# Key and value projection: context halves turned by transposing DMAs instead of fp32 transposes on TensorE

## The chip, the cores and the metric

The kernel runs on one core of a Trainium2 chip, in one launch. The metric is the device time of the launch in microseconds (us), lower is better. Matmuls run on TensorE (PE in the profile), elementwise work on VectorE (DVE), ScalarE (ACT) and GpSimd (POOL); SyncE (SP) issues all the transfers in the part that matters here.

## What is computed

The reference is one layer of a perceiver on 512 latent rows of width 512 and a context of 8192 rows of width 384: a cross attention with 16 heads, an MLP, a local self attention, and a feed-forward part with weights quantised to fp4. The change touches only the projection of the context to keys and values:

```python
k = (y @ Wk + bk).reshape(B, M, NUM_HEADS, HEAD_DIM)   # y: 8192 x 384, Wk, Wv: 384 x 512
v = (y @ Wv + bv).reshape(B, M, NUM_HEADS, HEAD_DIM)
```

## The kernel before

**Stages.** Four stages follow each other: project (keys, values, queries, and the fp4 weights on the side), attend (the cross attention), local (the self attention), ffn. The change is in project alone.

**Blocks.** The 8192 context rows are cut into NB = 16 blocks of 512 rows, y[:, u] of 128 partitions by 4 rows by 384, with u = block mod 2. Two blocks make one turn of a loop, which stands out of line for the first and the last pair and in a hardware loop (Fori) for pairs 1 to 6. fp32 accuracy is kept by splitting each operand in two fp16 halves, hi and lo, and adding three products: hi·hi, hi·lo, lo·hi.

**One block on each engine.** TensorE needs the context with its 384 columns on the partitions. In `turn_y` (line 588) it turns a block with 12 transposes of 128x128 in fp32 (line 593) into the PSUM tensor yT_ps. ACT copies yT_ps to yT_hi in fp16 (`y_high`, line 458), DVE subtracts to get yT_lo (`y_low`, line 513). `keys` (lines 611 to 613) then does 36 matmuls of 512 columns in four groups g; ACT writes each group as kf and k_hi (lines 449, 451), DVE makes k_lo (line 509). `values` (lines 627 to 629) does 36 more, and ACT copies each v out (line 465). TensorE's order is keys of block b, transposes of block b+1 (`next_y`), values of block b.

**Buffers.** yT_hi and yT_lo have two slots; k_ps and v_ps two banks each; yT_ps one set of three banks.

**SP's queue.** For a block, `block_dmas` (line 336) issues, in this order: the load of y for block b+2 (line 340, once block b's slot u is free), after a wait for all k_hi and k_lo of the block eight stores to k_scratch (lines 347, 348), and after a wait for the four v the store to v_scratch (line 350). After the second block of a pair come three stores and three loads of the fp4 side work (lines 361, 357). All are on one queue, q1.

**Side work.** DVE and POOL quantise the feed-forward weights in units (`scales`, `rounder`, `add`, `subtract`, `halves`), spread between DVE's k_lo and y_lo steps. It is why DVE reaches a k_lo late in some blocks.

**A transfer of the same kind.** In the local stage SP issues six transposing transfers (line 1434), each turning a 1408x512 fp16 matrix (1.44 MB) from DRAM into SBUF.

Of the kernel before, what the change touches and what calls it, by code (L numbers as in the profile page):

```python
# [22 lines left out]
ALU = mybir.AluOpType  # L23
# [3 lines left out]
F16 = mybir.dt.float16  # L27
# [102 lines left out]
def perceiver(nc, a, out):  # L130

    with ExitStack() as whole:
# [111 lines left out]
        with ExitStack() as st:  # L244
# [10 lines left out]
            yT_hi = sb("yT_hi", [P, 2, CK, BLK], F16)  # L255
            yT_lo = sb("yT_lo", [P, 2, CK, BLK], F16)
# [12 lines left out]
            w_whole = sb("w_whole", [P, UN])  # L269
            w_out = sb("w_out", [P, 3, 2, UN], F16)  # L270

            yT_ps = ps("yT_ps", [P, CK, BLK])
            k_ps = ps("k_ps", [P, 2, BLK])
            v_ps = ps("v_ps", [P, 2, D])

# [19 lines left out]
            yT_ready = sem("yT_ready")  # L295
            yhi_ready = sem("yhi_ready")
            ylo_ready = sem("ylo_ready")
            k_ready = sem("k_ready")
# [25 lines left out]
            def _(sp):  # L324
# [8 lines left out]
                sp.dma_start(y[:, 1], y_view[1]).then_inc(y_in[1], 16)  # L333
                sp.dma_start(b2[:], a["L0_xattn_b2"].partition_broadcast(P)).then_inc(b2_in, 16)

                def block_dmas(i, u, last):
                    if not last:

                        wait(sp, yT_ready, 2 * i + u + 1)
                        sp.dma_start(y[:, u], y_view[2 * i + u + 2]).then_inc(y_in[u], 16)  # L340

                    wait(sp, klo_ready, (2 * i + u + 1) * G)
                    wait(sp, khi_ready, (2 * i + u + 1) * G)
                    for s in range(HG):
                        rows = slice(s * HD, (s + 1) * HD)
                        keys = bass.ds((2 * i + u) * BLK, BLK)
                        sp.dma_start(k_hi_view[s, :, :, keys], k_hi[rows, u]).then_inc(k_out[u], 16)
                        sp.dma_start(k_lo_view[s, :, :, keys], k_lo[rows, u]).then_inc(k_out[u], 16)
                    wait(sp, vs_ready, (2 * i + u + 1) * BT)
                    sp.dma_start(v_view[:, :, bass.ds((2 * i + u) * BT * HD, BT * HD)],  # L350
                                 v[:, u].rearrange("p h t d -> p h (t d)")).then_inc(v_out[u], 16)
# [12 lines left out]
                for w in range(3):  # L364
                    sp.dma_start(w_in[:, w], w_flat[w][:, 0:UN]).then_inc(w_unit_in[w], 16)
                sp.dma_start(wq[:], a["L0_xattn_Wq"].rearrange("(k p) n -> p k n", p=P)).then_inc(wq_in, 16)
                def two_blocks(i):
                    block_dmas(i, 0, False)
                    block_dmas(i, 1, False)
                    for w in range(3):  # L370
                        unit_store(i, w)
                        unit_load(i + 1, w)
# [5 lines left out]
                for i in range(HG):  # L378
# [2 lines left out]
                    sp.dma_start(heads[0:HD, i], q_hi[rows]).then_inc(q_stacked, 16)  # L381
                    sp.dma_start(heads[HD:2 * HD, i], q_hi[rows]).then_inc(q_stacked, 16)
                    sp.dma_start(heads[2 * HD:3 * HD, i], q_lo[rows]).then_inc(q_stacked, 16)
                with sp.Fori(1, NB // 2 - 1) as i:
                    two_blocks(i)
                block_dmas(NB // 2 - 1, 0, True)
                block_dmas(NB // 2 - 1, 1, True)
# [42 lines left out]
            def _(act):  # L430
                layer_norm_scalar(act, var_ready, sd_ready, 1)

                act.wait_ge(yT_ready, 1)
                nc.scalar.activation(yT_hi[:, 0], yT_ps[:], ACT.Copy).then_inc(yhi_ready, 1)
# [18 lines left out]

                def y_high(i, u):

                    wait(act, yT_ready, 2 * i + u + 2)
                    wait(act, v_ready, (2 * i + u) * BT)
                    nc.scalar.activation(yT_hi[:, 1 - u], yT_ps[:], ACT.Copy).then_inc(yhi_ready, 1)

                def values_out(i, u):  # L460
                    for t in range(BT):
# [27 lines left out]
            def _(dve):  # L489
# [6 lines left out]
                nc.vector.tensor_tensor(yT_lo[:, 0], yT_ps[:], yT_hi[:, 0], ALU.subtract).then_inc(ylo_ready, 1)  # L496
# [88 lines left out]

            @block.tensor
            def _(pe):
                def turn_y(b, u):

                    pe.wait_ge(y_in[u], b)  # L590
                    for t in range(BT):
                        for c in range(CK):
                            last = nc.tensor.transpose(yT_ps[:, c, t * P:(t + 1) * P], y[:, u, t, c * P:(c + 1) * P],
                                                       ident[:])
                    last.then_inc(yT_ready, 1)

                pe.wait_ge(x_in, 32)
                turn_y(16, 0)
                pe.wait_ge(wsplit_hi, 1)
                pe.wait_ge(wsplit_lo, 1)  # L600

                def keys(i, u):
                    wait(pe, yhi_ready, 2 * i + u + 1)
                    wait(pe, ylo_ready, 2 * i + u + 1)
                    for g in range(G):
                        n = (2 * i + u) * G + g

                        wait(pe, khi_ready, n - 1 if g >= 2 else (2 * i + u) * G)
                        cols = slice(g * P, (g + 1) * P)
                        for k in range(CK):  # L610
                            nc.tensor.matmul(k_ps[:, g % 2], w_hi[:, 0, k, cols], yT_hi[:, u, k], start=k == 0, stop=False)  # L611
                            nc.tensor.matmul(k_ps[:, g % 2], w_hi[:, 0, k, cols], yT_lo[:, u, k], start=False, stop=False)  # L612
                            last = nc.tensor.matmul(k_ps[:, g % 2], w_lo[:, 0, k, cols], yT_hi[:, u, k], start=False,  # L613
                                                    stop=k == CK - 1)
                        last.then_inc(k_ready, 1)

                def values(i, u):
                    if isinstance(i, int) and i == 0 and u == 0:
                        pe.wait_ge(wsplit_hi, 2)
                        pe.wait_ge(wsplit_lo, 2)  # L620
                    for t in range(BT):
                        n = (2 * i + u) * BT + t

                        wait(pe, vs_ready, n - 1 if t >= 2 else (2 * i + u) * BT)
                        cols = slice(t * P, (t + 1) * P)
                        for k in range(CK):
                            nc.tensor.matmul(v_ps[:, t % 2], yT_hi[:, u, k, cols], w_hi[:, 1, k], start=k == 0, stop=False)  # L627
                            nc.tensor.matmul(v_ps[:, t % 2], yT_hi[:, u, k, cols], w_lo[:, 1, k], start=False, stop=False)  # L628
                            last = nc.tensor.matmul(v_ps[:, t % 2], yT_lo[:, u, k, cols], w_hi[:, 1, k], start=False,  # L629
                                                    stop=k == CK - 1)  # L630
                        last.then_inc(v_ready, 1)

                def next_y(i, u):
                    wait(pe, ylo_ready, 2 * i + u + 1)

                    turn_y(16 * (i + 1 + u), 1 - u)
# [12 lines left out]
                for k in range(DK):  # L649
                    if k >= 2:  # L650
                        pe.wait_ge(turned_out, k - 1)
                    for t in range(TT):
                        last = nc.tensor.transpose(v_ps[:, k % 2, t * P:(t + 1) * P], xn_q[:, t, k * P:(k + 1) * P], ident[:])
                    last.then_inc(turned, 1)
                pe.wait_ge(turned_out, DK)
                pe.wait_ge(wq_in, 16)
                for g in range(G):
                    if g >= 2:
                        pe.wait_ge(qhi_ready, g - 1)
                    for k in range(DK):  # L660
# [8 lines left out]
                next_y(i, 0)  # L669
                values(i, 0)  # L670
                keys(i, 1)
                values(i, 1)
# [1286 lines left out]
```

## Time and profile before

| | |
|---|---|
| median of 3 runs | 1485.82 us (1484.34 to 1488.38) |
| profiled execution | 1484.56 us, of which the span is 1482.8 us |
| mean granted TensorE clock | 0.955 |
| busy share of the span: PE, DVE, ACT, POOL | 91%, 76%, 55%, 54% |
| project stage in the span | from 0 to about 330 us |
| 12 transposes of a block on TensorE | 1.47 us busy |
| transfers of queue q1 | 129264 packets, 138.08 MB |

The engines run side by side, so busy shares don't add. The share of an engine is a mean over stages that differ; what counts for the change is what TensorE does, and waits for, between 8 and 321 us. Matmul durations overlap in the records (0.38 us each, started every 0.215 us), so the pitch of their starts is read, not the duration.

### The profile page before, as it was taken

The page shows a single profiled execution, that of the slowest core. Times are in us where ns is not written, and L with a number is a line of the kernel's source. Part 1 is how long each engine was busy: PE and PEld are TensorE (multiplying, and loading weights), DVE is VectorE, ACT ScalarE, POOL GpSimd, SP SyncE. Part 2 cuts the span into 40 slices and gives each one's busy share as a digit, 9 for nine tenths or more (in the row PEclk, how much of TensorE's full clock was granted, in tenths as well). Part 3 has the DMA queues.
Part 4 walks back from the last instruction along what each step waited for, and adds up shares of the span by engine and source line. Part 5 has one row for each costly group of instructions (what it writes and reads, how often), then busy time and mean ns, then how long its engine had stood idle before and what let it go on. Part 6 is the DMA issues. An engine that isn't in the chain of part 4 may idle for free. (4 is left out here: it accounts for less than half of the span.)

```text
span 1482.8 us, 43758 instructions
## 1 busy us (share of the span) xinstructions
PE 1356.4 (91%) x16736; PEld 651.1 (44%) x16736; DVE 1123.3 (76%) x1834; ACT 808.7 (55%) x1529; POOL 799.0 (54%) x307
## 2 busy tenths in 40 slices
PE   6999999968999999999999999999999897885898
PEld 3444444421344444444444444444444443453444
DVE  7477777768888887887887878878886654676797
ACT  3454444430566776666766766767667722474211
POOL 2122222232599898997997988979987001100111
PEclk9999999985899999999999999999999998898899
DMA  6578787765033222122212212221210030770000
GB/s 232 166 199 224 211 227 215 226 170 148 22 125 89 71 69 67 36 70 69 70 36 71 68 40 60 68 67 36 70 57 27 4 135 0 165 155 1 0 8 22
DMA packets 129452, 140.76 MB, mean 95 GB/s; under 512 B 44848, under 2 KB 110256, under 8 KB 127216
## 3 DMA queue, kind: packets, MB, share of 16 engines
q1 hardware_dynamic: 129264, 138.08, 32.8%
q8 instruction: 139, 2.28, 0.6%
q14 instruction: 49, 0.40, 0.1%
HBM read 77.23 MB, written 44.17 MB: 82 GB/s over the span
## 5 line engine op out<-in xcount | busy, mean ns | idle before, releaser
L1168 DVE TENSOR_REDUCE attend_part_max<-attend_banks 128x1 f32<-128x512 f32 x1024 | 635.9, 683 | 132.0 <-PE attend_banks L903 130.3
L1131 ACT ACTIVATE attend_prob<-attend_banks 128x512 f32<-128x512 f32 x1024 | 531.4, 603 | 234.9 <-PE attend_banks L955 229.6
L1316 POOL TENSOR_TENSOR early<-early,attend_prob 128x1024 f32<-128x1024 f32 x210 | 618.8, 2947 | 34.8 <-ACT attend_prob L1131 5.9
L903 PE MATMUL attend_banks<-attend_k_stack,attend_q_pre 96*32 96x512 f16 x4096 | 423.4, 401 | 31.1 <-DMA attend_k_stack<-k_scratch 16.4
L955 PE MATMUL attend_banks<-attend_q_now,attend_k_stack 97*32 97x512 f16 x4096 | 362.2, 386 | 14.3 <-ACT attend_prob L1131 14.3
L966 PE MATMUL attend_banks<-attend_prob,attend_vh 128*32 128x512 f32 x2048 | 265.2, 594 | 0.0
L955 PEld LDWEIGHTS attend_banks<-attend_q_now,attend_k_stack 97*32 97x32 f16 x4096 | 112.2, 97 | 164.1 <-ACT attend_prob L1131 104.5
L903 PEld LDWEIGHTS attend_banks<-attend_k_stack,attend_q_pre 96*32 96x32 f16 x4096 | 112.4, 96 | 126.6 <-DVE attend_part_max L1168 39.2
L977 PEld LDWEIGHTS attend_banks<-attend_prob,ones 128*32 128x32 f32 x3048 | 87.5, 109 | 159.5 <-issue 159.5
L977 PE MATMUL attend_banks<-attend_prob,ones 128*32 128x128 f32 x3048 | 126.9, 272 | 0.0
L413 POOL TENSOR_TENSOR project_w_whole<-project_grid,project_qscale 128x704 f32<-128x704 f32 x24 | 35.5, 1481 | 128.7 <-DVE project_grid L538 128.7
L1312 POOL TENSOR_TENSOR early<-attend_prob 128x1536 f32<-128x1536 f32 x15 | 53.4, 3559 | 89.6 <-ACT attend_prob L1131 89.6
L407 POOL TENSOR_TENSOR project_qn<-early,project_qinv 128x704 f32<-128x704 f32 x24 | 41.8, 1740 | 97.6 <-DVE project_qinv L524 94.1
L449 ACT ACTIVATE project_kf<-project_k_ps,project_bk 128x512 f32<-128x512 f32 x64 | 44.0, 687 | 86.1 <-PE project_k_ps L613 47.8
L627 PE MATMUL project_v_ps<-project_w_hi,project_yT_hi 128*128 128x512 f16 x192 | 73.6, 383 | 11.8 <-ACT project_v L465 11.8
L611 PE MATMUL project_k_ps<-project_yT_hi,project_w_hi 128*128 128x512 f16 x192 | 73.5, 383 | 6.8 <-DVE project_w_lo L499 5.0
L966 PEld LDWEIGHTS attend_banks<-attend_prob,attend_vh 128*32 128x32 f32 x2048 | 62.6, 111 | 35.5 <-issue 4.7
L612 PE MATMUL project_k_ps<-project_yT_lo,project_w_hi 128*128 128x512 f16 x192 | 73.6, 383 | 0.0
L628 PE MATMUL project_v_ps<-project_w_lo,project_yT_hi 128*128 128x512 f16 x192 | 73.5, 383 | 0.0
L629 PE MATMUL project_v_ps<-project_w_hi,project_yT_lo 128*128 128x512 f16 x192 | 73.4, 382 | 0.0
L613 PE MATMUL project_k_ps<-project_yT_hi,project_w_lo 128*128 128x512 f16 x192 | 73.4, 382 | 0.0
L465 ACT ACTIVATE project_v<-project_v_ps 128x512 f32<-128x512 f32 x64 | 37.7, 601 | 63.0 <-PE project_v_ps L629 63.0
(160 smaller groups left out, 1423.5 us busy)
## 6 DMA issues: line engine op xcount, KB each, us to landing
v_scratch<-project_v SPq DMA_DIRECT2D x16, 1024.0 KB, 5.7
attend_k_stack<-k_scratch SPq DMA_DIRECT2D x64, 256.0 KB, 3.5
attend_vh<-v_scratch SPq DMA_DIRECT2D x16, 1024.0 KB, 5.2
early<-in_ctx_dram SPq DMA_DIRECT2D x16, 768.0 KB, 7.4
k_scratch<-project_k_hi SPq DMA_DIRECT2D x64, 128.0 KB, 2.7
k_scratch<-project_k_lo SPq DMA_DIRECT2D x64, 128.0 KB, 2.9
attend_k_stack<-k_scratch SPq DMA_DIRECT2D x64, 128.0 KB, 3.5
late<-in_L_xattn_W_dram SPq DMA_DIRECT2D x2, 2048.0 KB, 10.7
```

Source lines behind the costliest of these rows:

```text
L611: nc.tensor.matmul(k_ps[:, g % 2], w_hi[:, 0, k, cols], yT_hi[:, u, k], start=k == 0, stop=False)
L612: nc.tensor.matmul(k_ps[:, g % 2], w_hi[:, 0, k, cols], yT_lo[:, u, k], start=False, stop=False)
L613: last = nc.tensor.matmul(k_ps[:, g % 2], w_lo[:, 0, k, cols], yT_hi[:, u, k], start=False, stop=k == CK - 1)
L627: nc.tensor.matmul(v_ps[:, t % 2], yT_hi[:, u, k, cols], w_hi[:, 1, k], start=k == 0, stop=False)
L628: nc.tensor.matmul(v_ps[:, t % 2], yT_hi[:, u, k, cols], w_lo[:, 1, k], start=False, stop=False)
L903: last = nc.tensor.matmul(pre_ps[c * HD:(c + 1) * HD, bank, :], q_pre[0:KROWS, s, queries], k_stack[0:KROWS, s, part * BLK:(part + 1) * BL ...
L955: last = nc.tensor.matmul(s_ps[c * HD:(c + 1) * HD, s_bank[n], :], k_stack[0:KROWS + 1, s, keys], q_now[0:KROWS + 1, s, :], start=True, st ...
L966: last = nc.tensor.matmul(pv_ps[t * HD:(t + 1) * HD, :], vh[:, s, BT * q + t, :], prob[:, q % PSLOTS, t, :], start=q == 0, stop=q == QUADS ...
L977: last = nc.tensor.matmul(den_ps[t * HD:(t + 1) * HD, 0:P], ones[:], prob[:, q % PSLOTS, n, t * P:(t + 1) * P], start=q == 0 and n == summ ...
L1131: nc.scalar.activation(prob[:, q % PSLOTS, t, :], s_ps[:, s_bank[BT * q + t]], ACT.Exp, scale=SCALE).then_inc(p_ready, 1)
L1168: nc.vector.tensor_reduce(part_max[:, s, j, part:part + 1], pre_ps[:, bank], AX.X, ALU.max).then_inc(pre_read, 1)
L1316: nc.gpsimd.tensor_tensor(sums, sums, prob[:, q % PSLOTS, 0:n], ALU.add).then_inc(pool_summed, 1)
```

## The change

The split is done before the turning. ACT makes y_hi and DVE y_lo from y as it lies in SBUF, both in fp16 and in two slots of their own. SP then issues two transposing transfers within SBUF, y_hi to yT_hi and y_lo to yT_lo (384 KB each), in place of TensorE's 12 transposes. yT_ps, `next_y` and TensorE's `turn_y` are gone; `keys` waits on the transfers' semaphore yT_in. SP's loop over the middle pairs is written out in place of Fori. The values' weights are now taken as yT_hi[:, u, t, k]; matmuls keep their number and shapes.

```diff
+            y_hi = sb("y_hi", [P, 2, BT * C], F16)
+            y_lo = sb("y_lo", [P, 2, BT * C], F16)
+            yT_hi = sb("yT_hi", [P, 2, BT, CK, P], F16)
+            yT_lo = sb("yT_lo", [P, 2, BT, CK, P], F16)
-            yT_ps = ps("yT_ps", [P, CK, BLK])
...
+                def turn_y(b, u):
+
+                    wait(sp, yhi_ready, b + 1)
+                    sp.dma_start(yT_hi[:, u].rearrange("p t c n -> p (t c) n"), y_hi[:, u], transpose=True).then_inc(yT_in[u], 16)
+                    wait(sp, ylo_ready, b + 1)
+                    sp.dma_start(yT_lo[:, u].rearrange("p t c n -> p (t c) n"), y_lo[:, u], transpose=True).then_inc(yT_in[u], 16)
...
                 def block_dmas(i, u, last):
                     if not last:
 
-                        wait(sp, yT_ready, 2 * i + u + 1)
+                        wait(sp, ylo_ready, 2 * i + u + 1)
                         sp.dma_start(y[:, u], y_view[2 * i + u + 2]).then_inc(y_in[u], 16)
 
                     wait(sp, klo_ready, (2 * i + u + 1) * G)
...
                         sp.dma_start(k_lo_view[s, :, :, keys], k_lo[rows, u]).then_inc(k_out[u], 16)
+                    if not (last and u == 1):
+
+                        wait(sp, v_ready, (2 * i + u) * BT)
+                        turn_y(2 * i + u + 1, 1 - u)
                     wait(sp, vs_ready, (2 * i + u + 1) * BT)
...
                 sp.dma_start(wq[:], a["L0_xattn_Wq"].rearrange("(k p) n -> p k n", p=P)).then_inc(wq_in, 16)
+                turn_y(0, 0)
...
-                with sp.Fori(1, NB // 2 - 1) as i:
+                for i in range(1, NB // 2 - 1):
                     two_blocks(i)
...
                 def y_high(i, u):
 
-                    wait(act, yT_ready, 2 * i + u + 2)
-                    wait(act, v_ready, (2 * i + u) * BT)
-                    nc.scalar.activation(yT_hi[:, 1 - u], yT_ps[:], ACT.Copy).then_inc(yhi_ready, 1)
+                    wait(act, y_in[1 - u], 16 * (i + 1 + u))
+                    wait(act, yT_in[1 - u], 32 * (i + u))
+                    nc.scalar.activation(y_hi[:, 1 - u], y[:, 1 - u].rearrange("p t c -> p (t c)"),
+                                         ACT.Copy).then_inc(yhi_ready, 1)
...
                 def y_low(i, u):
                     wait(dve, yhi_ready, 2 * i + u + 2)
-                    nc.vector.tensor_tensor(yT_lo[:, 1 - u], yT_ps[:], yT_hi[:, 1 - u], ALU.subtract).then_inc(ylo_ready, 1)
+                    nc.vector.tensor_tensor(y_lo[:, 1 - u], y[:, 1 - u].rearrange("p t c -> p (t c)"), y_hi[:, 1 - u],
+                                            ALU.subtract).then_inc(ylo_ready, 1)
...
                 def keys(i, u):
-                    wait(pe, yhi_ready, 2 * i + u + 1)
-                    wait(pe, ylo_ready, 2 * i + u + 1)
+                    wait(pe, yT_in[u], 32 * (i + 1))
...
                     for u in range(2):
                         keys(i, u)
-                        next_y(i, u)
                         values(i, u)
```

TensorE at the end of block 0's keys and the start of its values, before:

```order
37 L612 MATMUL project_k_ps<-project_yT_lo,project_w_hi 128x512
38 L613 MATMUL project_k_ps<-project_yT_hi,project_w_lo 128x512
39 L593 MATMUL project_yT_ps<-ident,early 128x128 [waits project_y_in1,project_ylo_ready]
40 L593 MATMUL project_yT_ps<-ident,early 128x128 x11
41 L627 MATMUL project_v_ps<-project_w_hi,project_yT_hi 128x512 [waits project_wsplit_lo,project_wsplit_hi]
```

and the same place with the change:

```order
35 L617 MATMUL project_k_ps<-project_yT_lo,project_w_hi 128x512
36 L618 MATMUL project_k_ps<-project_yT_hi,project_w_lo 128x512
37 L631 MATMUL project_v_ps<-project_w_hi,project_yT_hi 128x512 [waits project_wsplit_lo,project_wsplit_hi]
```

The twelve transposes are gone from TensorE's order. SP's order in block 2, with the change (`early` is the area that holds y):

```order
58 L348 DMA early<-in_ctx_dram 128x1536 [waits project_ylo_ready]
59 L355 DMA k_scratch<-project_k_hi 32x4x512 [waits project_khi_ready,project_klo_ready]
60 L356 DMA k_scratch<-project_k_lo 32x4x512
...
65 L355 DMA k_scratch<-project_k_hi 32x4x512
66 L356 DMA k_scratch<-project_k_lo 32x4x512
67 L340 DMA_TRANSPOSE project_yT_hi<-project_y_hi 128x12x128 [waits project_yhi_ready,project_v_ready]
68 L342 DMA_TRANSPOSE project_yT_lo<-project_y_lo 128x12x128 [waits project_ylo_ready]
69 L362 DMA v_scratch<-project_v 128x16x128 [waits project_vs_ready]
```

The two turns of block 3 stand behind the eight key stores of block 2 and ahead of the store of its values.

## Rows read from the trace of the kernel before

**Rows 1.** The page's busy times: engine, us, share, instructions; further engines
```profile
PE 1356.4 (91%) x16736; PEld 651.1 (44%) x16736; DVE 1123.3 (76%) x1834; ACT 808.7 (55%) x1529; POOL 799.0 (54%) x307
```

**Rows 2.** Waits, 40 to 325 us: who waited for what, us, times, longest
```profile
DVE project_amax L518 <- DMA early<-in_L_ffn_w_gate_dram: 25.2, 6, 5.0
...
PE project_v_ps L627 <- ACT project_v L465: 11.8, 6, 3.2
```

**Rows 3.** Groups by line, 0 to 430 us: busy us, mean ns; idle before
```profile
L627 PE MATMUL project_v_ps<-project_w_hi,project_yT_hi 128*128 128x512 f16 x192 | 73.6, 383 | 11.8 <-ACT project_v L465 11.8
...
L593 PE MATMUL project_yT_ps<-ident,early 128*128 128x128 f32 x192 | 24.9, 282 | 8.6 <-DMA early<-in_ctx_dram 8.6
```

**Rows 4.** PE's timeline: start, length, line; block starts and one pass of transposes
```profile
34.95 0.38 PE L611 MATMUL project_k_ps<-project_yT_hi,project_w_hi 128*128 128x512 f16 x1
...
42.72 1.47 PE L593 MATMUL project_yT_ps<-ident,early 128*128 128x128 f32 x12
44.02 0.38 PE L627 MATMUL project_v_ps<-project_w_hi,project_yT_hi 128*128 128x512 f16 x1
...
71.59 0.39 PE L611 MATMUL project_k_ps<-project_yT_hi,project_w_hi 128*128 128x512 f16 x1 [1.75 <-ACT project_q_hi L483]
...
305.14 0.38 PE L611 MATMUL project_k_ps<-project_yT_hi,project_w_hi 128*128 128x512 f16 x1
```

**Rows 5.** Timeline from the end of a block's keys to its key stores
```profile
169.17 1.47 PE L593 MATMUL project_yT_ps<-ident,early 128*128 128x128 f32 x12
...
169.95 0.68 ACT L451 ACTIVATE project_k_hi<-project_k_ps,project_bk 128x512 f16<-128x512 f32 x1
...
172.06 0.69 DVE L509 TENSOR_TENSOR project_k_lo<-project_kf,project_k_hi 128x512 f16<-128x512 f32 x1
...
172.66 1.75 DVE L513 TENSOR_TENSOR project_yT_lo<-project_yT_ps,project_yT_hi 128x1536 f16<-128x1536 f32 x1
172.91 0.33 SPq L347 DMA_DIRECT2D k_scratch<-project_k_hi  x1
...
176.50 0.46 SPq L348 DMA_DIRECT2D k_scratch<-project_k_lo  x1
```

**Rows 6.** Transposing transfers of the local stage: by line, to landing, and their queue
```profile
L1434 SPq DMA_TRANSPOSE turned_area<-fp_gate x2: 5452/5684/5915, 1284.0 to 1289.5; - x2
...
turned_area<-fp_gate SPq DMA_TRANSPOSE x2, 8.3
...
q1 hardware_dynamic: 34075, 8.73, 100.9%
```

**Rows 7.** Stretches: length, busy of five engines, PEclk, DMA share, GB/s
```profile
154.00:156.00 2.00, 0.18 (x1) 0.11 (x2) 1.77 (x4) 2.00 (x3) 0.00 (x0) 1.00 0.19 80
156.00:158.00 2.00, 2.00 (x7) 0.80 (x6) 1.81 (x3) 0.25 (x1) 0.00 (x0) 0.60 0.00 0
158.00:160.00 2.00, 2.00 (x7) 0.71 (x5) 2.00 (x3) 0.60 (x1) 0.00 (x0) 0.55 0.65 142
...
175.00:176.00 1.00, 1.00 (x6) 0.49 (x5) 1.00 (x2) 0.16 (x1) 0.00 (x0) 1.00 0.98 198
```

**Rows 8.** DMA issues, 100 to 300 us: count, KB each, us to landing
```profile
k_scratch<-project_k_lo SPq DMA_DIRECT2D x44, 128.0 KB, 2.9
```

**Rows 9.** Timeline of the start, and Wq's issue with its time to landing
```profile
late<-in_L_xattn_Wq_dram SPq DMA_DIRECT2D x1, 1024.0 KB, 10.2
...
10.90 0.48 SPq L366 DMA_DIRECT2D late<-in_L_xattn_Wq_dram  x1
...
12.88 1.76 DVE L496 TENSOR_TENSOR project_yT_lo<-project_yT_ps,project_yT_hi 128x1536 f16<-128x1536 f32 x1
...
16.41 0.59 PE L611 MATMUL project_k_ps<-project_yT_hi,project_w_hi 128*128 128x512 f16 x1 [5.04 <-DVE project_w_lo L499]
```

**Rows 10.** DVE on SBUF data: a group of lines, and one operation twice
```profile
L534 DVE TENSOR_TENSOR project_qs<-project_qn,project_qr 128x704 f32<-128x704 f32 x24 | 21.3, 887 | 0.3
...
162.90 1.96 DVE L545 SCALAR_TENSOR_TENSOR project_w_out<-project_w_whole,project_w_out 128x704 f16<-128x704 f32 x1
...
174.88 0.89 DVE L545 SCALAR_TENSOR_TENSOR project_w_out<-project_w_whole,project_w_out 128x704 f16<-128x704 f32 x1
```

More of the change, by code:

```diff
@@ L254, in perceiver @@
             q_lo = sb("q_lo", [P, G, T], F16)
-            yT_hi = sb("yT_hi", [P, 2, CK, BLK], F16)
-            yT_lo = sb("yT_lo", [P, 2, CK, BLK], F16)
+            y_hi = sb("y_hi", [P, 2, BT * C], F16)
+            y_lo = sb("y_lo", [P, 2, BT * C], F16)
+            yT_hi = sb("yT_hi", [P, 2, BT, CK, P], F16)
+            yT_lo = sb("yT_lo", [P, 2, BT, CK, P], F16)
             kf = sb("kf", [P, 2, BLK])
@@ L294, in perceiver @@
             q_stacked = sem("q_stacked")
-            yT_ready = sem("yT_ready")
+            yT_in = [sem(f"yT_in{u}") for u in range(2)]
             yhi_ready = sem("yhi_ready")
@@ L431, in _ @@
                 layer_norm_scalar(act, var_ready, sd_ready, 1)
-                act.wait_ge(yT_ready, 1)
-                nc.scalar.activation(yT_hi[:, 0], yT_ps[:], ACT.Copy).then_inc(yhi_ready, 1)
+                act.wait_ge(y_in[0], 16)
+                nc.scalar.activation(y_hi[:, 0], y[:, 0].rearrange("p t c -> p (t c)"), ACT.Copy).then_inc(yhi_ready, 1)
                 for w in range(2):
@@ L495, in _ @@
                 dve.wait_ge(yhi_ready, 1)
-                nc.vector.tensor_tensor(yT_lo[:, 0], yT_ps[:], yT_hi[:, 0], ALU.subtract).then_inc(ylo_ready, 1)
+                nc.vector.tensor_tensor(y_lo[:, 0], y[:, 0].rearrange("p t c -> p (t c)"), y_hi[:, 0],
+                                        ALU.subtract).then_inc(ylo_ready, 1)
                 for w in range(2):
@@ L512, in y_low @@
                     wait(dve, yhi_ready, 2 * i + u + 2)
-                    nc.vector.tensor_tensor(yT_lo[:, 1 - u], yT_ps[:], yT_hi[:, 1 - u], ALU.subtract).then_inc(ylo_ready, 1)
+                    nc.vector.tensor_tensor(y_lo[:, 1 - u], y[:, 1 - u].rearrange("p t c -> p (t c)"), y_hi[:, 1 - u],
+                                            ALU.subtract).then_inc(ylo_ready, 1)
                 def scales(i, w):
@@ L587, in _ @@
             def _(pe):
[L588 to L598, printed above, removed]
                 pe.wait_ge(wsplit_hi, 1)
@@ L610, in keys @@
                         for k in range(CK):
-                            nc.tensor.matmul(k_ps[:, g % 2], w_hi[:, 0, k, cols], yT_hi[:, u, k], start=k == 0, stop=False)
-                            nc.tensor.matmul(k_ps[:, g % 2], w_hi[:, 0, k, cols], yT_lo[:, u, k], start=False, stop=False)
-                            last = nc.tensor.matmul(k_ps[:, g % 2], w_lo[:, 0, k, cols], yT_hi[:, u, k], start=False,
+                            nc.tensor.matmul(k_ps[:, g % 2], w_hi[:, 0, k, cols], yT_hi[:, u, :, k], start=k == 0, stop=False)
+                            nc.tensor.matmul(k_ps[:, g % 2], w_hi[:, 0, k, cols], yT_lo[:, u, :, k], start=False, stop=False)
+                            last = nc.tensor.matmul(k_ps[:, g % 2], w_lo[:, 0, k, cols], yT_hi[:, u, :, k], start=False,
                                                     stop=k == CK - 1)
@@ L624, in values @@
                         wait(pe, vs_ready, n - 1 if t >= 2 else (2 * i + u) * BT)
-                        cols = slice(t * P, (t + 1) * P)
                         for k in range(CK):
-                            nc.tensor.matmul(v_ps[:, t % 2], yT_hi[:, u, k, cols], w_hi[:, 1, k], start=k == 0, stop=False)
-                            nc.tensor.matmul(v_ps[:, t % 2], yT_hi[:, u, k, cols], w_lo[:, 1, k], start=False, stop=False)
-                            last = nc.tensor.matmul(v_ps[:, t % 2], yT_lo[:, u, k, cols], w_hi[:, 1, k], start=False,
+                            nc.tensor.matmul(v_ps[:, t % 2], yT_hi[:, u, t, k], w_hi[:, 1, k], start=k == 0, stop=False)
+                            nc.tensor.matmul(v_ps[:, t % 2], yT_hi[:, u, t, k], w_lo[:, 1, k], start=False, stop=False)
+                            last = nc.tensor.matmul(v_ps[:, t % 2], yT_lo[:, u, t, k], w_hi[:, 1, k], start=False,
                                                     stop=k == CK - 1)
                         last.then_inc(v_ready, 1)
-                def next_y(i, u):
-                    wait(pe, ylo_ready, 2 * i + u + 1)
-                    turn_y(16 * (i + 1 + u), 1 - u)
                 def two_blocks(i):
@@ L668, in _ @@
                 keys(i, 0)
-                next_y(i, 0)
                 values(i, 0)
```

## The prediction

> **What bounds the kernel now.** I read the page's busy times first: TensorE works 91% of the span [rows 1]. That is a mean over stages, so I went on to the waits of the projection, 40 to 325 us. TensorE's one repeated wait there is for a copy of v, 11.8 us in six times [rows 2], once in each pair of blocks of the loop; behind it stands DVE, which had waited for a weight load (25.2 us, six times) and so gave the last k_lo late. Otherwise the matmuls follow each other: TensorE sets the pace of the projection. The groups of lines give the size of the work [rows 3]: 192 transposes take 24.9 us busy. TensorE's timeline gives what they hold on its path: the pass that starts at 42.72 lets the values start at 44.02, so 1.3 us a block [rows 4]. The same timeline gives the pace: block 2 starts at 71.59 and block 15 at 305.14, 13 periods of 17.96 us. A half block is 36 matmuls; from 34.95 to 42.72 that is 7.77 us. What is taken away is therefore at most 16 x 1.3 = 21 us, and the question is whether the new path from one block's end of keys to the next block's turned halves fits beneath the 7.77 us of values.
>
> **The new path, step by step.** SP issues the turns of block b+1 behind the eight key stores of block b. I take the steps from the block whose keys end at 169.17 [rows 5].
> 1. From the end of keys to the first key store: 169.17 to 172.91, 3.74 us. Bounds: 2.2 us if DVE takes up the last k_lo at once (k_hi ends at 170.63, k_lo takes 0.69), and some 5 us more in an even block if the weight load still comes late [rows 2]. I take 3.74, an ordinary block's.
> 2. Eight key stores: 172.91 to 176.96, 4.05 us. SP's Fori is written out, which drops a register move at each store; the stores are 0.5 us apart in the page's straight-line blocks too, so I count nothing for it.
> 3. The two turns. Before has no turn within SBUF, but it has six from DRAM by the same kind of instruction [rows 6]: 1.44 MB (5632 rows of 256 B; the queue's 34075 packets are about six times that) is issued in 5.68 us and lands 8.3 us after its issue began, so 2.6 us after the issue ended. One turn here is 1536 rows of 256 B, 0.273 of that: 1.55 us of issue. Two turns are 3.1 us, and the second lands 2.6 us later, 5.8 us with the gap between them. Bounds: 3 us if turns within SBUF land as fast as the 128 KB stores do (2.9 us [rows 8]); 9 us if issue costs twice as much from SBUF. I take 5.8, nearest in kind. The key stores don't lengthen this much: they keep the DMA engines busy 0.98 at 198 GB/s [rows 7], so 1 MB is through about when SP reaches the turns plus 1.7 us, and 0.79 MB of turned data behind it at the 240 GB/s or so of the six (1.44 MB in about 6 us) gives the same landing within 1 us.
>
> Sum from the end of keys to the landing: 3.74 + 4.05 + 5.8 = 13.6 us, against 7.77 us of values. TensorE gains the 1.3 us of its transposes and then stands still for 5.8 us.
>
> A rule of the Trainium skill stands against that price. Its page "Advanced Engine Details and Errata", section "X-Bar Transpose (TRN2)", expects transposing DMAs as fast as ordinary ones, 350 to 400 GB/s. The rows show less, 0.79 MB in 3.1 us; by the rule the two turns would move in about 2.1 us, an estimate from that page, and the total would come out some 15 us lower. The measured rate decides here.
>
> **The clock.** In the stretch 154 to 156 TensorE does almost nothing; in the next two stretches of 2 us its granted clock is 0.60 and 0.55, near the lower of its levels, 1.2 GHz, and seven matmuls fit where eleven would start otherwise [rows 7]. Some eight matmuls go at half pace, 8 x 0.215 = 1.7 us lost. That followed an idle time of about 2 us. I expect the same after each idle time of 5.8 us. Bounds: 0 and 1.9.
>
> **Period.** 7.77 (keys) + 1.7 + 13.6 = 23.1 us, against 17.96: +5.1. The old waits of 11.8 us are inside the 17.96 and vanish beneath the new wait.
>
> **Where the others go.** y_high and y_low have the same size as before but read SBUF. By the subtraction of 704 columns in 0.887 us [rows 10], 1536 columns take 1.93 us against 1.75. One operation on SBUF data beside POOL shows 1.96 for 0.89 us [rows 10], so up to 4.2 us. Cover: y_low must end when SP asks for the second turn, 5.6 us after k_lo. It costs nothing; without that cover, up to 2.6 us a block. The load of y for block b+2 is freed a little later (after the split and not after TensorE), a whole period ahead of its use. The store of v and the fp4 loads stand behind the turns on SP, some 3 us later against keys' end, but the period is 5 us longer, so the weight load comes no later against DVE's need. DMA traffic grows by 0.79 MB a block, and the longer period takes it in.
>
> **The sum.**
> - Blocks 2 to 14, 13 periods: 13 x 5.1 = +67.
> - Block 0: from 16.41 to 34.95 before, 18.5; now 23.1: +4.6.
> - Block 1: its follower's turn is hidden by the projection of queries (52 to 71 us); 1.3 saved, 1.7 lost to the clock: +0.4. Block 15: +1.7.
> - The start. Block 0's keys start at 16.41, waiting for w_lo and not for y [rows 9]. y_lo is ready at 14.64. Its turn stands behind Wq's load, issued at 10.90 and landed at 21.1; with 3.1 us of turned data it lands at about 24: +7.6. Bounds: at 18.8 (+2.4) if the queue is no obstacle, and 25.
> Together +81 on the profiled execution of 1484.56 us, which is 1565. The median of the runs shown is 1.3 us above that execution, well within what counts as no change (0.3%, 4.5 us, about what a measurement of this kernel can tell). After 330 us nothing changes.
>
> **Rivals.**
> - *The new wait is short.* DVE gives the last k_lo at once (-1.5), the clock isn't lowered (-1.7), the turns take 4.8 (-1.0): 4.2 less in 14 periods and 3 less at the start, 1503; one or two of the three, 1520 to 1540. For it: DVE has more room in a longer period. Against: the clock fell after about 2 us of idle time. 12%.
> - *A turn costs more.* Twice the issue from SBUF adds 3.1 us to 14 periods and the start: 1611; with the weight load also late in the seven even blocks, 5 us each, 1646. For it: source rows come from 128 partitions and not from DRAM, which no row shows. 21%.
> - *Each 128x128 tile has a price of its own.* 1.44 MB is 44 such tiles in 5.68 us, 0.13 us each, so 24 tiles are 3.1 us. If tiles from SBUF went one after the other, each with about half the 2.6 us tail, 1.3 us, then 24 would be 31 us, 25 us more in 15 turns: about 1950. 2%. The Trainium skill, page "VectorE: DVE Perf Modes", section "The three transpose paths", gives 1309 ns for a 128x128 turn by DMA alone and 390 ns on TensorE; by it the change loses outright. The rows of the six transfers speak against it for a stream of tiles.
> - *It is faster.* The turn lands beneath the values, and 1.3 us go in 15 blocks: 1484.6 - 19.5 + 2.4 = 1467. That decides from the point where lag, stores and turns are 7.77 us together. The lag and the stores are 7.79 by themselves. It needs the lag at 2.2, the stores at 0.33 us apart (their issue alone, 2.6) and both turns landed in 2.9. 3%.
>
> **How the numbers follow.** The forecast, a wait in each block of 4 to 8 us with the clock lowered, 1540 to 1600: 62%, and its centre 1565 is the predicted time. The range takes in most of the cheaper and of the dearer case: 1520 to 1630. Faster by over 0.3% only by the last rival, 3%; within 0.3%, 1%; slower 96%.
>
> **What would show it.** TensorE's longest wait in the projection would be the first key matmul on the DMA of yT, 15 times, 4 to 8 us each; the two turns issue in about 1.5 us each, right behind the last key store, and land 2.6 us after; the granted clock in the projection falls well below 1 after each wait; the project stage ends near 400 us. A period near 23 us confirms the sum; a wait under 2 us, or turns that issue in over 3 us each, would show the step that is wrong.

## The result, and the profile after

The changed kernel takes 1581.2 us (median of 4 runs, 1575.04 to 1584.5) against 1487.1 before: 1.064 times as long (95% interval 1.061 to 1.066), 94 us more. 1565 was forecast, within 1520 to 1630. The profiled execution took 1583.66 us. Each ratio in the experiments below is to runs of the kernel before that were measured beside them (medians 1484.5 to 1485.9 us).

The page of the changed kernel, busy times, and a group of lines (busy, mean ns, idle time before and what ended it):

```profile
PE 1364.5 (86%) x16544; PEld 637.2 (40%) x16544; DVE 1133.6 (72%) x1834; ACT 808.7 (51%) x1529; POOL 795.3 (50%) x307
...
L616 PE MATMUL project_k_ps<-project_yT_hi,project_w_hi 128*128 128x512 f16 x192 | 85.2, 444 | 117.4 <-DMA project_yT_lo<-project_y_lo 115.7
```

TensorE's share falls from 91% [rows 1] to 86% of a longer span. Its busy time rises by 8 us although the transposes (24.9 us busy [rows 3]) are gone, because matmuls at the lower clock last longer. The first key matmul stands behind 115.7 us of waiting for the turned low half. It has a mean of 444 ns where the values' matmul before, at the same shape, had 383 [rows 3]: part of the keys runs at the lower clock.

TensorE's timeline after, rows that follow a wait (start, length, line; in brackets the idle time and what ended it), from several stretches:

```profile
23.91 0.58 PE L616 MATMUL project_k_ps<-project_yT_hi,project_w_hi 128*128 128x512 f16 x1 [23.91 <-DMA project_yT_lo<-project_y_lo]
47.06 0.61 PE L616 MATMUL project_k_ps<-project_yT_hi,project_w_hi 128*128 128x512 f16 x1 [6.17 <-DMA project_yT_lo<-project_y_lo]
...
83.95 0.39 PE L616 MATMUL project_k_ps<-project_yT_hi,project_w_hi 128*128 128x512 f16 x1 [1.65 <-ACT project_q_hi L498]
106.47 0.60 PE L616 MATMUL project_k_ps<-project_yT_hi,project_w_hi 128*128 128x512 f16 x1 [6.80 <-DMA project_yT_lo<-project_y_lo]
...
179.41 0.60 PE L616 MATMUL project_k_ps<-project_yT_hi,project_w_hi 128*128 128x512 f16 x1 [6.17 <-DMA project_yT_lo<-project_y_lo]
...
396.21 0.61 PE L616 MATMUL project_k_ps<-project_yT_hi,project_w_hi 128*128 128x512 f16 x1 [7.57 <-DMA project_yT_lo<-project_y_lo]
```

Every block but the first and block 2 (83.95, behind the queries) begins with a wait of 6.2 to 7.6 us. Block 2 begins at 83.95 and block 15 at 396.21: 13 periods of 24.0 us in place of 17.96 [rows 4]. Before, the same block 15 began at 305.14, so 91 of the 99 us between the two profiled executions are there by then. The attend stage begins 93 us later, at 430.5 us (337.3 before). The prediction's list of signs had the project stage end near 400, but its own sum puts the start of attend at 337 + 81 = 418; 12 us more than that were measured. The stage ends 98 us later; those 5 us within it have no cause that I found, and the runs of one kernel differ by as much.

One chain of the changed kernel, ahead of 179.41, from the timeline (the values' first matmul after the keys, then DVE, then SP's queue):

```profile
165.30 0.38 PE L631 MATMUL project_v_ps<-project_w_hi,project_yT_hi 128*128 128x512 f16 x1
...
168.18 0.69 DVE L525 TENSOR_TENSOR project_k_lo<-project_kf,project_k_hi 128x512 f16<-128x512 f32 x1
168.79 2.94 DVE L529 TENSOR_TENSOR project_y_lo<-early,project_y_hi 128x1536 f16<-128x1536 f32 x1
...
168.90 0.33 SPq L355 DMA_DIRECT2D k_scratch<-project_k_hi  x1
...
172.36 0.52 SPq L356 DMA_DIRECT2D k_scratch<-project_k_lo  x1
172.98 1.64 SPq L340 DMA_TRANSPOSE project_yT_hi<-project_y_hi  x1
174.66 2.63 SPq L342 DMA_TRANSPOSE project_yT_lo<-project_y_lo  x1
177.33 0.58 SPq L362 DMA_DIRECT2D v_scratch<-project_v  x1
```

Issues of the changed kernel, 100 to 300 us (count, us from issue to landing):

```profile
project_yT_hi<-project_y_hi SPq DMA_TRANSPOSE x9, 4.6
project_yT_lo<-project_y_lo SPq DMA_TRANSPOSE x9, 4.4
```

| step of the chain | forecast | this block |
|---|---|---|
| keys (block that began at 155.46, to 165.30) | 7.77 + 1.7 | 9.84 |
| keys' end to first key store | 3.74 | 3.60 |
| eight key stores | 4.05 | 4.08 |
| two turns, first issue to TensorE's start | 5.8 | 6.43 |
| period | 23.1 | 23.95 |

The eight key stores take the same time in the written-out loop as in Fori, so writing it out gave nothing.

The subtraction that makes y_lo took 2.94 us in this block beside other work; it ended at 171.73, before SP asked for the low turn at 174.66, so its cover held.

### The profile page after: what moved, and what is told of

Same layout as the page of the kernel before. It is cut to its first block and busy times, and to the rows that moved or that the text cites. A ratio compares the mean times of both kernels' runs of the same rounds, so it can differ in the third digit from the quotient of the medians.

```text
span 1581.9 us, 43036 instructions
## 1 busy us (share of the span) xinstructions
PE 1364.5 (86%) x16544; PEld 637.2 (40%) x16544; DVE 1133.6 (72%) x1834; ACT 808.7 (51%) x1529; POOL 795.3 (50%) x307
## 5 line engine op out<-in xcount | busy, mean ns | idle before, releaser
L963 PE MATMUL attend_banks<-attend_prob,attend_vh 128*32 128x512 f32 x2048 | 268.6, 600 | 0.0
L616 PE MATMUL project_k_ps<-project_yT_hi,project_w_hi 128*128 128x512 f16 x192 | 85.2, 444 | 117.4 <-DMA project_yT_lo<-project_y_lo 115.7
L525 DVE TENSOR_TENSOR project_k_lo<-project_kf,project_k_hi 128x512 f16<-128x512 f32 x64 | 51.3, 802 | 123.2 <-ACT project_k_hi L465 121.4
L617 PE MATMUL project_k_ps<-project_yT_lo,project_w_hi 128*128 128x512 f16 x192 | 84.3, 439 | 0.0
L618 PE MATMUL project_k_ps<-project_yT_hi,project_w_lo 128*128 128x512 f16 x192 | 82.7, 431 | 0.0
L616 PEld LDWEIGHTS project_k_ps<-project_yT_hi,project_w_hi 128*128 128x128 f16 x192 | 21.1, 110 | 152.9 <-issue 116.2
```

The costliest lines, as they stand in the source:

```text
L963: last = nc.tensor.matmul(pv_ps[t * HD:(t + 1) * HD, :], vh[:, s, BT * q + t, :], prob[:, q % PSLOTS, t, :], start=q == 0, stop=q == QUADS ...
```

## The experiments

Theory: the turns stand at the end of a serial chain (last k_lo, key stores, turns) that is longer than the values, and TensorE waits out the rest. Rivals: the turning is itself too slow, or its traffic is what costs; or the clock is.

**1. Key stores out of the chain (e2).** The two turns stand ahead of the eight stores in SP's order.

```diff
                     wait(sp, khi_ready, (2 * i + u + 1) * G)
+                    if not (last and u == 1):
+                        wait(sp, v_ready, (2 * i + u) * BT)
+                        turn_y(2 * i + u + 1, 1 - u)
                     for s in range(HG):
...
-                    if not (last and u == 1):
-                        wait(sp, v_ready, (2 * i + u) * BT)
-                        turn_y(2 * i + u + 1, 1 - u)
```

> The changed kernel with one edit in SP's order: the two turns stand ahead of the eight key stores, still behind the wait for the last k_lo. Theory: the 4.1 us of the key stores leave the chain, y_lo (1.75 us) is ready when the first turn has been issued; TensorE's wait falls from 6.5 to about 2.5 us in 14 blocks, the clock still falls after some of them: 1581 - 57 = 1524 us, 1510 to 1535. Rival (the turns wait for something else, such as the data of the stores or their own slowness): above 1560.

Measured: 1535.4 us, ratio to before 1.032 (1.029 to 1.036): 46 us less than the changed kernel by one move in SP's order. Its waits, 5 to 400 us:

```profile
PE project_k_ps L616 <- DMA project_yT_lo<-project_y_lo: 47.1, 15, 23.8
DVE project_amax L535 <- DMA early<-in_L_ffn_w_gate_dram: 42.1, 6, 8.3
PE project_v_ps L631 <- ACT project_v L480: 29.4, 6, 6.6
```

Without the 23.8 at the start, 23 us of waits on turned halves are left of 92. The theory's mechanism holds. The gain is 46 us and not 57 because the theory left the old wait out: values waiting for a copy behind DVE, which waits for the gate load, came back, none in the changed kernel, 11.8 us in the kernel before [rows 2], 29.4 here. Without the stores ahead of them most turns issue in 1.3 to 1.6 us each (median 1.4 and 1.6), as the prediction's step 3 had it; behind the stores, in the changed kernel, the medians are 2.0 and 1.9.

**2. One turn (e3).**

```diff
-                    sp.dma_start(yT_lo[:, u].rearrange("p t c n -> p (t c) n"), y_lo[:, u], transpose=True).then_inc(yT_in[u], 16)
+                    if b == 0:
+                        sp.dma_start(yT_lo[:, 0].rearrange("p t c n -> p (t c) n"), y_lo[:, u], transpose=True).then_inc(yT_in[u], 16)
```

> The changed kernel without the turn of the low half from block 1 on (all blocks read block 0's turned low half, so the low half of the context is left out there). Theory: a turn costs its issue, about 2.0 us in the chain, 14 times exposed: 1581 - 28 = 1553 us. Rival (the landing time is the price and the issue is hidden): less than 10 us gained. Rival (turns share bandwidth so that each costs half of the 6.6 us): 1581 - 46 = 1535.

Measured: 1553.4 us (ratio 1.045, 1.043 to 1.047), as the theory had it. One turn is worth its issue of about 2 us; the wait that is left, 4.4 us or so (62.5 us in 14), is the landing time that a single turn keeps.

**3. The clock (e4).**

```diff
+                def warm():
+                    for _ in range(26):
+                        nc.tensor.matmul(warm_ps[:], w_hi[:, 0, 0, 0:P], w_hi[:, 0, 0], start=True, stop=True)
...
                         values(i, u)
+                        warm()
```

> The changed kernel with 26 matmuls of 512 columns on TensorE after the values of each of 15 blocks, into a PSUM bank that nobody reads: 5.6 us of work in a wait of 6.5. Theory: TensorE is busy through the wait, the granted clock stays at 1.0 in the projection and the 1.9 us that the keys lose at the lower clock come back in 14 blocks, less the block ahead of the queries, where the extra work adds 5.6: 1581 - 27 + 6 = 1560 us. Rival (the clock is hidden or falls anyway): 1581 or more.

Measured: 1574.9 us (ratio 1.061, 1.059 to 1.063), 6 us less than the changed kernel and not 21; the changed kernel's own runs spread over 9.5 us. The mean granted clock rose from 0.926 to 0.953. Block starts, from TensorE's timeline of this kernel; the last line is from its waits, 5 to 400 us:

```profile
109.93 0.39 PE L617 MATMUL project_k_ps<-project_yT_hi,project_w_hi 128*128 128x512 f16 x1 [0.86 <-DMA project_yT_lo<-project_y_lo]
...
131.93 0.39 PE L617 MATMUL project_k_ps<-project_yT_hi,project_w_hi 128*128 128x512 f16 x1 [0.68 <-DMA project_yT_lo<-project_y_lo]
...
156.03 0.61 PE L617 MATMUL project_k_ps<-project_yT_hi,project_w_hi 128*128 128x512 f16 x1 [2.71 <-DMA project_yT_lo<-project_y_lo]
...
179.20 0.39 PE L617 MATMUL project_k_ps<-project_yT_hi,project_w_hi 128*128 128x512 f16 x1 [0.36 <-DMA project_yT_lo<-project_y_lo]
...
DVE project_amax L536 <- DMA early<-in_L_ffn_w_gate_dram: 10.8, 6, 2.1
```

The odd block from 109.93 takes 22.0 us (24.7 in the changed kernel); the even one from 131.93, at full clock, takes 24.1 (24.3), and the next starts slow again. In even blocks DVE now waits for the gate load (10.8 us, six times; 1.3 us, once, in the changed kernel). Its chain starts at that landing and not at the keys, so faster keys win nothing there. The edit did only half of what it was meant to: from block 5 on every odd block still starts at the lower clock, after 2.4 to 2.7 us of idle time (keys 9.3 to 9.5 us). So the block from 109.93 is the only odd one that shows the clock given back, 2.7 us. In the profiled executions the attend stage begins 3.5 us earlier than in the changed kernel, and the extra matmuls ahead of the queries cost 3 us of their own. What the clock is worth in the other odd blocks stays open; neither the theory (1560) nor its rival (1581 or more) came out.

**4. The turns' traffic by itself (e5).** The kernel before, with two turns behind each block's key stores, into tensors that nobody reads.

```diff
+                    for j, half in enumerate((k_hi, k_lo)):
+                        sp.dma_start(junk[:, u, j], half[:, u, 0:CK].rearrange("p g n -> p (g n)"),
+                                     transpose=True).then_inc(k_out[u], 16)
```

> The kernel before, with two turns of the same size added on SP behind the key stores of each of 16 blocks, from k_hi and k_lo into tensors that nobody reads, and SP's loop written out. TensorE keeps its transposes. It prices the turns' traffic and issue time on SP by themselves. Theory (the loss is TensorE's wait and not traffic): SP is 4 us later in each block, which makes the fp4 loads later and TensorE's old wait in each pair longer by up to 4 us: 1487 to 1515 us. Rival (traffic and SP's time are the loss): above 1540.

Measured: 1509.8 us (ratio 1.017, 1.015 to 1.019). Nobody waits for these turns, and they cost 24 us: DVE's wait on the gate load goes from 25.2 to 41.4 us and TensorE's on v from 11.8 to 22.7 (six times each). In the kernel before only the wait that ends at 155.82 is followed by matmuls at half pace, 7 of them; here all six are, 49 in all. That is 42 more at 0.215 us, 9 us, and with the 10.9 us of waits it makes the 20 us by which blocks 2 to 14 take longer; the last 4 aren't placed. So traffic and SP's time are not free, as the theory said, but a quarter of the loss. This stands beside the chain and isn't to be added to it: in the changed kernel the longer period hides it.

**5. Turns issued early (e1).** ACT and DVE split block b+1 after block b's second key group, and SP issues the turns ahead of the wait on k_hi and k_lo. The lines taken from the old places are not shown.

```diff
                         nc.scalar.activation(k_hi[:, u, g], k_ps[:, g % 2], ACT.Identity, bias=bk[:, g:g + 1],
                                              scale=1.0 / WSCALE).then_inc(khi_ready, 1)
+                        if g == 1 and split:
+                            y_high(i, u)
...
                             key_low(i, u, g)
+                            if g == 1 and not (last and u == 1):
+                                y_low(i, u)
                             quantize(AFTER_KEYS[g])
...
+                    if not (last and u == 1):
+                        wait(sp, v_ready, (2 * i + u) * BT)
+                        turn_y(2 * i + u + 1, 1 - u)
                     wait(sp, klo_ready, (2 * i + u + 1) * G)
```

> The changed kernel, with the split of block b+1 done after the second key group of block b (on ScalarE and VectorE) and its two turns issued ahead of block b's key stores. Theory (the loss is the turns' place at the end of a serial chain, and not the turns): they are issued some 8 us after the keys begin and land within 5, before the values end at 15.5 us, so TensorE waits for no turn; 1.3 us a block is saved and only the start costs 7.5: 1465 to 1480 us. Rival (the turning itself, or its traffic, is too slow for the period of a block): the wait on the turned halves stays at 2 us or more and the time above 1510 us.

Measured: 1497.9 us (ratio 1.009, 1.006 to 1.011). The waits on turned halves are gone but for 3.7 us besides the start, so 83 of the 94 us were the place of split and turns in the order of work. Blocks without a wait now take 15.54 us (131.95 to 147.49), where before they took 16.85 (88.45 to 105.30): the 1.3 us of transposes that were to be won. It stayed 18 us above the theory's top. Its waits:

```profile
PE project_k_ps L616 <- DMA project_yT_lo<-project_y_lo: 27.5, 4, 23.8
DVE project_amax L535 <- DMA early<-in_L_ffn_w_gate_dram: 26.6, 6, 4.9
PE project_v_ps L631 <- ACT project_v L482: 22.6, 6, 4.3
```

The old wait is back and doubled: 10.8 us more than before, and 48 matmuls at half pace behind it in place of 7, another 8.8 us. Together that is the 18 us and a little more.

**6. The start (e6).** e1 with the load of Wq behind block 0's turns.

> The version with the early split and the turns ahead of the key stores (e1, 1497.9 us), with one more edit: the load of Wq is issued behind block 0's turns and not ahead of them. Theory of the start (block 0's turned halves land behind the data of the loads ahead of them): 1 MB less ahead, 3.5 us at the rate of the loads, so the keys start at 20 to 21 us and not at 23.8, and the time is 1494. Rival (the turn of the low half, which can't be issued before 14.6 us, sets it): no change.

Measured: 1497.5 us (ratio 1.008, 1.006 to 1.010). The keys do start earlier, at 21.47 and not at 23.84 (20 to 21 was expected). Block 15 begins only 1.0 us earlier, and the total, expected at 1494, didn't move by what the runs can tell.

**7 and 8. DVE's steps later (e7 on e6, e8 on the kernel before).** Both move DVE's side work in a pair's first block: the first two steps go from behind key groups 1 and 2 to behind 3 and 4, and the third goes behind y_low.

```diff
-                AFTER_KEYS = (1, 1, 1, 0)
-                AFTER_Y = (4, 5)
+                AFTER_KEYS = ((0, 0, 1, 1), (1, 1, 1, 0))
+                AFTER_Y = (5, 5)
```

> The version of e6 with VectorE's first two steps of fp4 side work in a pair's first block moved from behind the first and second key group to behind the third and fourth. In e1 VectorE waits 26.6 us for the gate load there, in six pairs, and TensorE 22.6 us for a copy of v behind it, at the lower clock afterwards. Theory: both go, 22.6 + 6 x 1.7 = 33 us from 1494, at best 1461; 1460 to 1472. Rival (VectorE has no slack and is late elsewhere): above 1480.

> The kernel before with the same move of VectorE's steps, and TensorE's transposes as they were. Its waits there are 11.8 us, and some 1.5 us each at the lower clock: 1486 - 11.8 - 9 = 1465 us, 1463 to 1475. With e7 it shows what the turns by DMA are worth when both have the better order: by the theory 15 x 1.3 = 20 us less the later start (4 us). Rival (TensorE's transposes cost nothing because another engine sets the pace): e7 and e8 are equal.

Measured: e7 1490.7 us (ratio 1.004, 1.003 to 1.006); e8 1475.7 us (ratio 0.994, 0.992 to 0.996). e8 takes 9 us off the kernel before: its wait on v is gone (1475.7 us, 0.7 above the 1463 to 1475 expected). With the better order on both sides the version with turns by DMA loses by 15, where the theory had it win by 16. Neither the theory nor its rival (equal) holds. e7 lies above the 1480 of its own rival too, but not for the reason given there: no wait on v is left, and the new waits are for turned halves, 24.8 us besides the start, all of them ahead of odd blocks (the expectations of e9 and e11 say even ones). Of the 15 us, 4.9 are the later start of block 0's keys, 21.31 against 16.45. e7's waits, and then its SP queue ahead of an even block's end:

```profile
PE project_k_ps L616 <- DMA project_yT_lo<-project_y_lo: 46.1, 8, 21.3
DVE project_amax L535 <- DMA early<-in_L_ffn_w_gate_dram: 9.7, 6, 1.9
```

```profile
115.16 1.76 DVE L529 TENSOR_TENSOR project_y_lo<-early,project_y_hi 128x1536 f16<-128x1536 f32 x1
...
117.64 0.51 SPq L369 DMA_DIRECT2D early<-in_L_ffn_w_down_dram  x1
118.19 1.05 SPq L348 DMA_DIRECT2D early<-in_ctx_dram  x1
119.34 2.98 SPq L340 DMA_TRANSPOSE project_yT_hi<-project_y_hi  x1
122.36 3.51 SPq L342 DMA_TRANSPOSE project_yT_lo<-project_y_lo  x1
```

```profile
128.07 0.60 PE L616 MATMUL project_k_ps<-project_yT_hi,project_w_hi 128*128 128x512 f16 x1 [3.96 <-DMA project_yT_lo<-project_y_lo]
```

y_lo is ready at 116.92. The turns stand behind six fp4 transfers and the load of y (2.9 MB), are issued in 3.0 and 3.5 us and not in 1.6 to 2.6, and TensorE starts 8.7 us after the first issue. All engines, 24 to 320 us, first in the kernel before and then in e7 (length, busy time of PE, PEld, DVE, ACT, POOL, granted clock, DMA share, GB/s):

```profile
24.00:320.00 296.00, 280.81 (x1351) 137.39 (x1350) 211.44 (x315) 142.15 (x214) 75.93 (x47) 0.99 0.71 199
```

```profile
24.00:320.00 296.00, 267.88 (x1165) 118.42 (x1163) 215.50 (x310) 142.84 (x215) 73.59 (x46) 0.97 0.95 240
```

At the shorter period the DMA engines are busy 0.95. That made a new theory: the turns wait behind other transfers' data.

**9 and 10. Less data (e9 on e7, e10 on e8).**

```diff
-                        sp.dma_start(y[:, u], y_view[2 * i + u + 2]).then_inc(y_in[u], 16)
+                        sp.dma_start(y[:, u, 0:2], y_view[2 * i + u + 2][:, 0:2]).then_inc(y_in[u], 16)
...
-                    sp.dma_start(w_in[:, w], w_flat[w][:, bass.ds(i * UN, UN)]).then_inc(w_unit_in[w], 16)
+                    sp.dma_start(w_in[:, w, 0:UN // 2], w_flat[w][:, bass.ds(i * UN, UN // 2)]).then_inc(w_unit_in[w], 16)
```

> The version of e7 with half the bytes in each later load of y and of the fp4 units (the other half of these inputs is left out and keeps the first block's values): 1.3 MB less for a pair of blocks, about what the turns add (1.6 MB), with the same number of transfers. In e7 TensorE still waits 25 us for turned halves, before even blocks, 2.4 to 5 us each, with the DMA engines busy 0.93. Theory (the turns wait behind the data of other transfers in SP's queue): the waits go and the time falls from 1490.7 to 1462 to 1468. Rival (the issue order and the time of SP alone make them late): above 1482.

> The version of e8 (TensorE's transposes, VectorE's steps later) with the same halved loads, as the reference for e9: TensorE sets its pace and the DMA engines are busy 0.72, so less traffic should change nothing but the small waits: 1470 to 1476 us. If e9 is below it, the turns by DMA are worth something where the queue has room.

Measured: e9 1472.0 us (ratio 0.991, 0.990 to 0.993), e10 1471.2 us (0.990, 0.989 to 0.992). Both leave out half of these inputs, so they only price the data. Taking away bytes gives the version with turns 19 us and the one without 4.5 (1470 to 1476 was expected of it). So the amount of data is what made e7 lose; whether it is the data ahead of the turns or the load on the DMA engines at large, these two don't tell apart. It isn't all: e9 still waits 11.8 us for turned halves besides the start (33.2 less 21.4), and comes out level with e10, 4 us above what was expected.

**11. Turns ahead of the load of y (e11 on e7).**

```diff
+                    if not (last and u == 1):
+                        wait(sp, v_ready, (2 * i + u) * BT)
+                        turn_y(2 * i + u + 1, 1 - u)
                     if not last:
                         wait(sp, ylo_ready, 2 * i + u + 1)
                         sp.dma_start(y[:, u], y_view[2 * i + u + 2]).then_inc(y_in[u], 16)
-                    if not (last and u == 1):
-                        wait(sp, v_ready, (2 * i + u) * BT)
-                        turn_y(2 * i + u + 1, 1 - u)
```

> The version of e7 with the two turns issued ahead of the load of y for the block after, in place of behind it: 0.77 MB and 1.2 us of issue less ahead of them. Theory of e9 (data ahead in the queue): the turns land 3 to 4 us earlier before even blocks, the waits of 25 us fall below 10, 1465 to 1475 us, level with e8 (1475.7) or below it. The danger is that y then comes late for the split: a new wait of ScalarE on y, and TensorE's wait on v behind it.

Measured: 1478.2 us (ratio 0.996, 0.994 to 0.997), 12 us less than e7 and 3 us outside the expected range. The waits fell from 24.8 to 16.1 us, and below 10 was expected; why turns are still late stays open. With the same bytes moved as in e7, this gain comes from what stands ahead of the turns. It is the best version with turns by DMA found here that does all the work, below the kernel before, 103 us below the change as made, and not below e8 with TensorE's transposes (1475.7).

## Why the prediction was right

- **What bounds the stage, and what can be won.** Right. The twelve transposes were worth 1.3 us a block, as e1's blocks of 15.54 against 16.85 us show, 21 in all.
- **The chain.** Right, step by step, as the table above shows. e2 and e1 show that it is the chain and not the turning: 46 us by a move in SP's order, 83 by splitting earlier as well.
- **Step 3, the two turns.** The mechanism held; the size was low: 5.8 forecast, 6.43 in the block above and 6.46 in the mean of 13. Taken from the local stage's transfers, the issue was 1.55 us a turn, and medians of 2.0 and 1.9 were seen (1.3 to 2.9 behind key stores); a turn landed 4.4 to 4.6 us after its issue began, not 4.2. The sentence that the key stores don't lengthen this much is where it was low: with the stores behind the turns (e2) the issue is 1.4 and 1.6. The pair of transfers it was taken from was also the quickest of three, 5.68 us of issue where the others took 6.0 and 6.3. This is most of the missing time: 13 periods of 24.0 and not 23.1 are 12 of the 16 us between forecast and median, 9 of them in the turns, 3 in lag and stores (8.06 for 7.79).
- **The other prices for a turn.** The Trainium skill's rate of 350 to 400 GB/s ("Advanced Engine Details and Errata", "X-Bar Transpose (TRN2)") would have put the forecast 15 us lower, farther off. The Trainium skill's 1309 ns for one 128x128 tile ("VectorE: DVE Perf Modes", "The three transpose paths"), paid for each tile in turn, would have put it near 1950. The trace agrees with neither for these transfers: a turn of 12 tiles landed in 4.4 to 4.6 us, and two (0.79 MB) took 6.43 us from first issue to TensorE's start.
- **The clock.** Right as a row: over blocks 2 to 14 the keys took 9.50 us in the mean (9.64 in those behind a wait), 9.47 forecast. But the ground for it was thin, and that the one row read was the one that fits is in part luck. That row follows the only one of the six waits before after which the clock fell; others of 3.16 and 2.05 us were followed by matmuls at full pace, 0.38 us each. They are these rows of the kernel before:

```profile
229.77 0.39 PE L627 MATMUL project_v_ps<-project_w_hi,project_yT_hi 128*128 128x512 f16 x1 [3.16 <-ACT project_v L465]
...
265.69 0.39 PE L627 MATMUL project_v_ps<-project_w_hi,project_yT_hi 128*128 128x512 f16 x1 [2.05 <-ACT project_v L465]
```

Also, "eleven would start otherwise" is misread: at 0.215 us a start, nine start in 2 us; the 1.7 us for eight matmuls stands without it. As a price that comes back when the clock does, it is not shown: e4 gave back 6 us and not 21, because in even blocks the chain starts at the gate load's landing, where the forecast took DVE's chain to follow the keys, and because most odd blocks kept the lower clock.
- **The start.** Forecast at 24, seen at 23.91; e6 confirms that Wq's data stood ahead of the turn.
- **The period hides the traffic.** Right for the change as made. It hid a second limit that no step of the prediction named: e5, e7 and e9 show that at the period the change was meant for, the queue's data makes the turns late.
- **The rival that it is faster** needed the turns to land beneath the values. e11 comes near that by another order of the same work (16.1 us of waits are left) and is 0.4% below before. But e11 also has DVE's steps later, which alone give 0.6% (e8), so no run shows the version with turns by DMA ahead of the one without, at the same order of DVE's steps.
- **The cheaper rival's prices.** Any one of its three savings alone gives 1541 to 1551 and not 1520 to 1540; the range and the forecast don't change by it.

## What to carry to other kernels

When work moves from an engine to a transfer, lay its whole new path, with every instruction queued ahead of it on the issuing engine, beside the time of the work that is to cover it; here lag and stores had used up the cover of 7.8 us before the first turn was issued. Then ask what the transfer meets at the faster pace that is hoped for and not at today's: with the DMA engines 71% busy before, 0.79 MB more a block found room at 24 us (73% busy) and hardly any at the pace of e7 (95%). And look first at the small wait that the profile already shows; moving DVE's steps won 9 us by itself, and the best placed turns together with that move 6.

## What the runs showed that I had not expected

- A turn's issue time is no constant: 1.3 us at the shortest, 1.3 to 2.9 behind the key stores, 3.0 and 3.5 where 2.9 MB of other transfers stood ahead (e7), 7.2 behind the loads at the start. In these rows it grows with the data issued just before; what SP waits for within an issue no trace here shows.

```profile
L340 SPq DMA_TRANSPOSE project_yT_hi<-project_y_hi x16: 1281/2312/7193, 11.3 to 306.6; - x16
```

That row is e1's first turn by line (shortest, median, longest in ns).
- Matmuls that only keep TensorE busy raise its clock and still win little: in e4, after idle times of 2.4 to 2.7 us, the keys ran slowly again (0.61 us a matmul at 156.03), and after 0.4 to 0.9 us they did not. The length of the idle time doesn't decide it alone: in e2 three waits of 2.3 us ahead of the keys were followed by slow matmuls and three were not, and in e7 one of 3.46 us was not.
